# Deformable sampling beside the attention: one bilinear corner moves from VectorE to ScalarE, and the output convolution takes two tiles at once

## The chip, the cores and the metric

One NeuronCore of a Trainium2 chip runs the whole program. The time is the device time of one execution in microseconds, and of several executions the median counts.

## What is computed

The input is x, four samples of 128 channels by 64 x 64 pixels in fp32. Four layers follow one another, each of the form x = x + layer(group_norm(x)).

```python
# layer 0: attention over the L = 4096 pixels of a sample (keys and values are the same)
q, k = Wq @ xf + bq, Wk @ xf + bk
attn = softmax(q.T @ k / sqrt(128));  out = xf + attn @ k.T
# layer 1: weights of 9 taps made from x by two small matmuls, times the dilated taps of x
# layer 2: 7x7 depthwise convolution, layer norm, 128 -> 512 -> 128 with gelu
# layer 3: deformable convolution, 9 taps
offset, mask = conv3x3(x)                       # 18 offsets, 9 masks for each pixel
py, px = y + dy_k + offset_y, x + dx_k + offset_x
val = c00*(1-ly)*(1-lx) + c01*(1-ly)*lx + c10*ly*(1-lx) + c11*ly*lx   # 4 gathered corners
out = relu(batch_norm(einsum('bckhw,ock->bohw', val * mask, weight)))
```

Layer 3 is what the change touches: for every pixel and each of the 9 taps, four corners of 128 channels are gathered, weighted and added, and the 9 sums go through a matmul with 9 weight matrices of 128 x 128.

## The kernel before, in words

**Samples and stages.** A sample is a tile of 128 channels by 4096 pixels in SBUF. `sample(n, dcn)` runs, on each engine's own queue, the group norm, `attention`, `layer1`, `layer2` and `layer3_prepare`. The deformable sampling of sample n-1 isn't done in its own turn: it is woven into the attention of sample n (`dcn` is true for n = 1, 2, 3). That of the last sample runs alone at the end (`tail_*`).

**Attention.** The 4096 queries are cut into 8 chunks of 512 (`NCH`), the 4096 keys into 32 tiles of 128 (`T`), which makes 256 steps (`STEPS`). In step `at` each engine does its piece, in this order in its queue:

- TensorE: `scores(at + 2)`, four matmuls of 512 columns in bf16 (lines 485 to 488) into one of two banks, once `exp_done` says that the bank has been read; `weigh_values(at - 1)`, twelve matmuls of 129 columns (line 519), the last four of them after VectorE and GpSimd have made the low part of the exponentials (`pl_v`, `pl_p`); `max_scores` for a later chunk, one matmul of 512 columns (line 446) into one of two banks, once VectorE has reduced the bank's former content (`mx_red`). The last 38 steps have no `max_scores`.
- ScalarE: `exponent(at)` (line 838).
- VectorE: `low_values(at + 1)` (line 1237) for 320 of 512 columns, then `max_reduce` (line 1177).
- GpSimd: `low_values(at + 1)` (line 1589) for the other 192 columns, then the gathers.

Once for each chunk TensorE also has `q_project` (line 409), `input_rows` (line 471) and `shift_rows` (line 457), and VectorE has `normalize` (lines 1192, 1198), `input_sum` (line 1186), `q_low` (line 1157) and `max_finish` (lines 1162 to 1166).

**Sampling.** The 4096 pixels are 32 tiles of 128. Tile j begins at step `begin(j) = 15 * j // 2`, so there is one tile in 7.5 steps, and `tile_at(at, offset)` gives the tile that is `offset` steps old. Nine indirect DMAs (line 1578, GpSimd) in steps -12 to -6 bring the patches: for each tap 4 corners x 128 channels for 128 pixels. The patches of a tile lie in one of four slots (`patches`: two in `G`, one in `regq`, one in `x_cur`, with a ninth tap of the latter two in `xl`). Then, by offset:

- 1 to 3, ScalarE `first_corner` (line 854): `val = corner 0 * weight`, nine instructions of 128 elements. 4 to 6, `second_corner` (line 862): corner 1 is scaled in its own place.
- 3 to 8, VectorE `interpolate`, 18 `scalar_tensor_tensor` (line 1214), three in a step: `val += corner 2 * weight`, then `val += corner 3 * weight`. 9: one addition of the whole tile, `val += corner 1` (line 1224, and line 1227 for the ninth tap in two slots of four), a drain, and `val_rdy`. `val` has two halves, by j % 2.
- 11 to 13, TensorE `dcn_transposes` (line 533), three in a step, into columns 0 to 383 of bank `TR[0]`. The first group waits for `val_rdy`, the others for `tr_ev`, which says that the group before has been copied out. 13 to 15, ScalarE `dcn_evacuate` (line 869), 384 columns. ScalarE runs about two steps ahead of TensorE, since `exponent(at)` needs only `scores(at)`.
- 14 to 16, TensorE `dcn_conv` (line 542), three of nine fp32 matmuls in a step, each with 128 columns, into columns 384 to 511 of the same bank. In the profile an fp32 matmul of this kind is two records. 18, ScalarE `dcn_result` (line 876); 20, for every fourth tile VectorE `dcn_finish` (line 1250) and a store.

The functions that the change touches follow, with the line numbers of the profile.

## Time and profile before

| | us |
|---|---|
| median of 3 runs (4402.11 to 4411.94) | 4408.24 |
| the profiled execution | 4407.83 |
| its span, first to last instruction | 4406.1 |

The page gives the busy time of each engine, the chain of work that ended last, and groups of instructions by line. The timeline lists single instructions with their starts. A record of a matmul is longer than the time to the next start, as matmuls are pipelined, so costs are taken from start to start. "PEld" is the weight load of TensorE. An "x3" after a row of the timeline says that three equal instructions are merged, and "[0.80 <- DVEq L1228]" that the engine sat idle for 0.80 us before this instruction, until VectorE's queue reached line 1228. Of the TensorE matmul rows a few per cent are missing, of the weight loads none that matters here.

### The profile page before, as it was taken

How to read it: one execution, taken by the hardware profiler on the slowest of the kernel's cores; microseconds unless marked ns; L12 is line 12 of the kernel's file. 1: busy time of each engine (PE TensorE's matmuls, PEld its weight loads, DVE VectorE, ACT ScalarE, POOL GpSimd, SP SyncE). 2: the span in 40 equal slices, each digit the busy share in tenths (PEclk: the TensorE clock that was granted, in tenths of full speed). 3: DMA queues.
4: the chain of work that ended last, by engine and by line, in shares of the span. 5: the costliest groups of instructions: out<-in, count | busy, mean ns of one | idle time of the engine just before them, and what ended most of it. 6: DMA issues, size and time to landing. Idle time of an engine off the chain costs nothing.

```text
span 4406.1 us, 76129 instructions
## 1 busy us (share of the span) xinstructions
PE 3694.5 (84%) x25784; PEld 2322.8 (53%) x26161; DVE 3455.3 (78%) x7009; ACT 2026.8 (46%) x4605; POOL 2220.1 (50%) x2457
## 2 busy tenths in 40 slices
PE   4999789879999869969999968978999977984555
PEld 2666434347776624436777733434777753433444
DVE  5999687579999768759999957848999967854666
ACT  2444432346666541236666742235666653222333
POOL 3444340058878550028877732007888834004775
PEclk9999899889999979989999988988999988986565
DMA  1000100154545300045554400034454520006775
GB/s 46 11 11 11 27 1 0 46 155 149 157 146 155 96 0 1 0 141 152 153 154 146 134 25 1 0 93 141 150 155 149 152 62 0 0 19 186 216 222 178
DMA packets 206462, 401.41 MB, mean 91 GB/s; under 512 B 23089, under 2 KB 121804, under 8 KB 204584
## 3 DMA queue, kind: packets, MB, share of 16 engines
q0 software_dynamic: 92160, 302.06, 22.9%
q1 hardware_dynamic: 113906, 94.92, 7.3%
q8 instruction: 197, 3.23, 0.3%
q14 instruction: 145, 1.19, 0.1%
q10 hardware_dynamic: 54, 0.01, 0.0%
HBM read 337.36 MB, written 59.53 MB: 90 GB/s over the span
## 4 chain that ended last, share of the span: by engine, by line
PE 44%; DVE 25%; issue 11%; POOL 10%; POOLq 4%; DVEq 3%; ACT 2%; DMA 1%; SPq 0%; ACTq 0%; another core or an unknown queue 0%
PE bank L657 11%; PE bank L519 8%; DVE val L1214 8%; DVE mxc L1177 6%; DVE xl L1237 4%; POOL G L1578 3%; DVE val L1224 2%; PE bank L683 2%; POOLq L1553 2%; PE bank L699 2%; PE bank L486 2%; PE bank L542 2%; PE bank L720 2%; PE bank L722 2%; PE bank L446 1%
## 5 line engine op out<-in xcount | busy, mean ns | idle before, releaser
L1589 POOL TENSOR_TENSOR xl<-pt 128x192 bf16<-128x192 f32 (+1 forms) x1024 | 683.4, 668 | 441.2 <-ACT pt L838 215.2
L838 ACT ACTIVATE pt<-bank 128x512 f32<-128x512 f32 x1024 | 608.8, 595 | 574.4 <-PE bank L488 317.3
L1578 POOL DMA_INDIRECT G<-patch_table,idx x576 | 590.9, 1026 | 202.5 <-issue 114.3
L519 PEld LDWEIGHTS bank<-vt,pt 128*128 128x128 bf16 x8192 | 549.5, 98 | 242.8 <-ACT pt L838 3.9
L1177 DVE TENSOR_REDUCE mxc<-bank 128x1 f32<-128x512 f32 x896 | 608.1, 680 | 38.0 <-PE bank L446 31.7
L519 PE MATMUL bank<-vt,pt 128*128 128x129 bf16 (+1 forms) x8192 | 633.7, 220 | 3.5 <-ACT osb L846 1.6
L1360 DVE SCALAR_TENSOR_TENSOR G<-xn,vec,G 128x512 f32<-128x512 f32 x736 | 521.6, 748 | 47.2 <-issue 40.7
L1237 DVE TENSOR_TENSOR xl<-pt 128x320 bf16<-128x320 f32 (+1 forms) x1024 | 500.1, 489 | 73.0 <-PE bank L519 53.8
L1563 POOL TENSOR_TENSOR rs<-ve,mhalf 128x4 f32<-128x4 f32 x32 | 36.6, 1143 | 820.1 <-ACT ve L974 820.1
L519 PE MATMUL bank<-vt,xl 128*128 128x129 bf16 x4096 | 401.7, 221 | 12.3 <-DVE xl L1237 11.6
L657 PE MATMUL bank<-vt,val 128*128 (+1 forms) x1152 | 373.2, 389 | 19.5 <-DVE xl L1152 19.5
L1214 DVE SCALAR_TENSOR_TENSOR val<-G,w,val 128x128 f32<-128x128 f32 x864 | 317.6, 419 | 4.4
L1578 POOL DMA_INDIRECT x_cur<-patch_table,idx x256 | 273.7, 1069 | 56.9 <-issue 48.4
L486 PE MATMUL bank<-ql,regk 128*128 128x512 bf16 x768 | 292.9, 381 | 5.0 <-issue 0.5
L487 PE MATMUL bank<-qh,regk 128*128 128x512 bf16 x762 | 290.8, 382 | 0.0
L1578 POOL DMA_INDIRECT regq<-patch_table,idx x256 | 258.7, 1011 | 61.7 <-issue 45.7
L519 PEld LDWEIGHTS bank<-vt,xl 128*128 128x128 bf16 x4096 | 273.4, 98 | 18.5 <-DVE xl L1237 16.7
L446 PE MATMUL bank<-regk,qh 128*128 128x512 bf16 x711 | 272.2, 384 | 12.5 <-DVE mxc L1177 9.3
L488 PE MATMUL bank<-m,ones 128*128 128x512 bf16 x738 | 281.5, 381 | 0.3
L485 PE MATMUL bank<-qh,regk 128*128 128x512 bf16 x678 | 258.5, 381 | 5.1 <-ACT m L817 2.3
L542 PE MATMUL bank<-valt,dcnw_s 128*128 128x128 f32 x1728 | 242.4, 276 | 1.6
L542 PEld LDWEIGHTS bank<-valt,dcnw_s 128*128 128x128 f32 x1728 | 233.9, 191 | 8.5 <-issue 1.5
(253 smaller groups left out, 7247.6 us busy)
## 6 DMA issues: line engine op xcount, KB each, us to landing
patch_table<-valt SPq DMA_DIRECT2D x64, 512.0 KB, 7.1
G<-patch_table,idx POOLq DMA_INDIRECT x576
x_cur<-in_x SPq DMA_DIRECT2D x4, 2048.0 KB, 8.4
xl<-in_x SPq DMA_DIRECT2D x32, 256.0 KB
attn_out<-ob SPq DMA_DIRECT2D x32, 256.0 KB
x_store<-x_cur SPq DMA_DIRECT2D x4, 2048.0 KB, 6.3
xr<-x_store SPq DMA_DIRECT2D x32, 256.0 KB, 4.6
out<-fo SPq DMA_DIRECT2D x32, 256.0 KB
```

The lines of the kernel that those rows point to most:

```text
L446: mm(MX[at % 2], qh[:, q0:q0 + 128], kh[:, mc * CH:(mc + 1) * CH], start=True, stop=True)\
L486: mm(bank, kh[:, tile], cols(ql, i % Q_RING), start=False, stop=False)
L519: last = mm(O[t // 2][:, c0:c0 + width], image[:, at % ring, t * 128:(t + 1) * 128], vhl[:, values, st, 0:width], start=(st == 0 and part ...
L542: last = mm(TR[0][:, 384:512], dcnw_s[:, k, :], valt[:, k, piece], start=(k == 0), stop=(k == K1 - 1))
L657: last = mm(as_rows(ST[u][:]), diag(k, part), shifted(c, k // 7 - 3, k % 7 - 3, image), start=(k == 0 and image is xh and part == 0), stop ...
L838: A(pt[:, at % PT_RING, :], ST[at % ST_RING] if n else ST_FIRST[at % 3], ACT.Exp, scale=SCALE).then_inc(s["exp_done"], 1)
L1177: v.reduce_max(mxc[:, t, mc:mc + 1], MX[at % 2], AX.X).then_inc(s["mx_red"], 1)
L1214: v.scalar_tensor_tensor(dst, src, w4[:, j, corner * K1 + k:corner * K1 + k + 1], dst, ALU.mult, ALU.add)
L1237: v.tensor_tensor(pl[:, at % PL_RING, first:CH], pt[:, at % PT_RING, first:CH], ph[:, at % PT_RING, first:CH], ALU.subtract).then_inc(s["p ...
L1360: v.scalar_tensor_tensor(acc, src, wgt, acc, ALU.mult, ALU.add)
L1578: g.indirect_dma_start(out=patches(j, k), out_offset=None, in_=table[:], in_offset=bass.IndirectOffsetOnAxis(ap=idx[:, j * K1 + k:j * K1 + ...
L1589: g.tensor_tensor(pl[:, at % PL_RING, 0:stop], pt[:, at % PT_RING, 0:stop], ph[:, at % PT_RING, 0:stop], ALU.subtract).then_inc(s["pl_p"], 1)
```

## The change

Nine more instructions of ScalarE scale corner 2 in its own place, as corner 1 is scaled already (`corner_scale`, which spreads 27 instructions over offsets 1 to 8). VectorE keeps nine `scalar_tensor_tensor` for corner 3 (offsets 4 to 6) and does two whole-tile additions, of corner 1 at offset 7 and of corner 2 at offset 9, each behind a wait (`c1_rdy`, `c2_rdy`) and a drain. The transposes come in five groups of two, two, two, two and one (offsets 11 to 15) into columns 0 to 255 of the bank, and each is evacuated by an instruction of 256 or 128 columns (offsets 13 to 17). The convolution runs for odd tiles alone, for both tiles of the pair, with 256 columns: five of the nine matrices at offset 16, four at offset 17. Its result is read at offset 19, `dcn_finish` comes at 21. The counters of the tail are renumbered, with nothing else changed there; those parts are left out.

```diff
@@ -41,7 +41,8 @@
 PATCH = 4 * C
 SCALE = float(C) ** -0.5
 STEPS = NCH * T
-SPT = 7
+SPT = 5
+TRR = 5
 X_COPY, X_ROWS, X_SUM = 10, 12, 13
 Q_NEXT, SHIFT = 18, 28
 LEAD, LEAD_FIRST = 6, 10
@@ -265,7 +266,7 @@
             "t_ps t_ev in_ve in_pow in_ready relu_rdy tl_rdy l1w l1p l1s l1a l1f "
             "diag_rdy dwp y_rdy ln_m ln_d ln_sq ln_v ln_ve ln_rs ln_dg ln_bc z_rdy hp gl mo me xa "
             "oc_ps oc_ev ot_ps ot_ev xs_rdy xt_ps xt_ev om_rdy em_rdy grid_rdy idx_rdy x3_out tbl_w "
-            "gat0 gat1 gat2 gat3 c1_rdy val_rdy tr_ps tr_ev conv_ps res_rdy xr_in fin fin_out tail_ps").split()}
+            "gat0 gat1 gat2 gat3 c1_rdy c2_rdy val_rdy tr_ps tr_ev conv_ps res_rdy xr_in fin fin_out tail_ps").split()}
 
         weights = ((wq_s[:], wq), (wk_s[:], wk), (l2w1_s[:], l2w1), (l2w2_s[:], l2w2), (offw_s, offw),
                    (offb_s[:], offb), (dcnw_s[:], dcnw), (vec[:], vecs))
@@ -382,7 +383,7 @@
         @block.tensor
         def _(pe):
             mm = nc.tensor.matmul
-            pe.sem_inc(s["tr_ps"], 4)
+            pe.sem_inc(s["tr_ps"], TRR + 1)
             for name in ("mo", "xt_ps", "ot_ps"):
                 pe.sem_inc(s[name], 2)
             pe.wait_ge(s["w_in"], 16 * WEIGHTS)
@@ -525,24 +526,25 @@
                 J = m * T + j
                 if r == 0:
                     pe.wait_ge(s["val_rdy"], J + 1 + 2)
-                    if j:
+                    if j and j % 2 == 0:
                         pe.wait_ge(s["res_rdy"], J)
-                else:
-                    pe.wait_ge(s["tr_ev"], 3 * J + r + 1)
-                for k in range(3):
-                    last = nc.tensor.transpose(TR[0][:, k * 128:(k + 1) * 128], val[:, j % 2, 3 * r + k, :],
+                if r or j % 2:
+                    pe.wait_ge(s["tr_ev"], TRR * J + r + 1)
+                for k in range(2 * r, min(2 * r + 2, K1)):
+                    last = nc.tensor.transpose(TR[0][:, k % 2 * 128:(k % 2 + 1) * 128], val[:, j % 2, k, :],
                                                ident[:])
                 last.then_inc(s["tr_ps"], 1)
 
             def dcn_conv(m, j, r):
-                piece = slice(j % TB * 128, (j % TB + 1) * 128)
+
+                piece = slice((j % TB - 1) * 128, (j % TB + 1) * 128)
                 if r == 0:
-                    pe.wait_ge(s["tr_ev"], 3 * (m * T + j + 1) + 1)
-                for k in range(3 * r, 3 * r + 3):
-                    last = mm(TR[0][:, 384:512], dcnw_s[:, k, :], valt[:, k, piece],
+                    pe.wait_ge(s["tr_ev"], TRR * (m * T + j + 1) + 1)
+                for k in range(5 * r, min(5 * r + 5, K1)):
+                    last = mm(TR[0][:, 256:512], dcnw_s[:, k, :], valt[:, k, piece],
                               start=(k == 0), stop=(k == K1 - 1))
-                if r == 2:
-                    last.then_inc(s["conv_ps"], 1)
+                if r == 1:
+                    last.then_inc(s["conv_ps"], 2)
 
             def attention(n, dcn):
                 lag = 5 if dcn else 2
@@ -590,12 +592,13 @@
                     if not dcn and r == IMAGE and i + 1 < NCH:
                         image_of_shift(i + 1)
                     if dcn:
-                        for part in range(3):
+                        for part in range(TRR):
                             j = tile_at(at, 11 + part)
                             if j is not None:
                                 dcn_transposes(n - 1, j, part)
-                            j = tile_at(at, 14 + part)
-                            if j is not None:
+                        for part in range(2):
+                            j = tile_at(at, 16 + part)
+                            if j is not None and j % 2:
                                 dcn_conv(n - 1, j, part)
                 weigh_values(n, STEPS - 1)
 
...
@@ -845,36 +848,31 @@
                 for h in range(2):
                     A(osb[:, h, :], O[h][:, 0:2 * (C + 1)], ACT.Copy).then_inc(s["o_evac"], 1)
 
-            def first_corner(m, j, part):
-
-                if part == 0:
-                    act.wait_ge(s["tr_ps"], 3 * (m * T + j) + 1)
+            def corner_scale(m, j, o):
+
+                corner, k = o // K1, o % K1
+                if o == 0:
+                    act.wait_ge(s["tr_ps"], TRR * (m * T + j) + 1)
                     act.wait_ge(gathered(j), landed(m, j))
-                for k in range(3 * part, 3 * part + 3):
-                    last = A(val[:, j % 2, k, :], patches(j, k)[:, 0:C], ACT.Copy, scale=w4[:, j, k:k + 1])
-                if part == 2:
-                    last.then_inc(s["c0_rdy"], 1)
-
-            def second_corner(m, j, part):
-
-                for k in range(3 * part, 3 * part + 3):
-                    src = patches(j, k)[:, C:2 * C]
-                    last = A(src, src, ACT.Copy, scale=w4[:, j, K1 + k:K1 + k + 1])
-                if part == 2:
-                    last.then_inc(s["c1_rdy"], 1)
+                src = patches(j, k)[:, corner * C:(corner + 1) * C]
+                op = A(val[:, j % 2, k, :] if corner == 0 else src, src, ACT.Copy,
+                       scale=w4[:, j, corner * K1 + k:corner * K1 + k + 1])
+                if k == K1 - 1:
+                    op.then_inc(s[f"c{corner}_rdy"], 1)
 
             def dcn_evacuate(m, j, r):
-                act.wait_ge(s["tr_ps"], 3 * (m * T + j) + r + 1 + 4)
+                act.wait_ge(s["tr_ps"], TRR * (m * T + j) + r + 1 + TRR + 1)
                 piece = slice(j % TB * 128, (j % TB + 1) * 128)
-                A(valt[:, 3 * r:3 * r + 3, piece], TR[0][:, 0:384].rearrange("p (k n) -> p k n", k=3), ACT.Copy)\
-                    .then_inc(s["tr_ev"], 1)
+                taps = min(2, K1 - 2 * r)
+                A(valt[:, 2 * r:2 * r + taps, piece],
+                  TR[0][:, 0:taps * 128].rearrange("p (k n) -> p k n", k=taps), ACT.Copy).then_inc(s["tr_ev"], 1)
 
             def dcn_result(m, j):
                 act.wait_ge(s["conv_ps"], m * T + j + 1)
-                if j % TB == 0:
+                if j % TB == 1:
                     act.wait_ge(s["fin_out"], 16 * (m * NCH + j // TB + 1))
-                A(fo[:, j % TB * 128:(j % TB + 1) * 128], TR[0][:, 384:512], ACT.Relu, bias=bn[:, 3:4],
-                  scale=bn[:, 2:3]).then_inc(s["res_rdy"], 1)
+                A(fo[:, (j % TB - 1) * 128:(j % TB + 1) * 128], TR[0][:, 256:512], ACT.Relu, bias=bn[:, 3:4],
+                  scale=bn[:, 2:3]).then_inc(s["res_rdy"], 2)
 
             def attention(n, dcn):
                 def values(c):
@@ -912,18 +910,16 @@
                     if not dcn and r == IMAGE + 1 and i + 1 < NCH:
                         image_copy(i + 1)
                     if dcn:
-                        for part in range(3):
+                        for part in range(TRR):
                             j = tile_at(at, 13 + part)
                             if j is not None:
                                 dcn_evacuate(n - 1, j, part)
-                            j = tile_at(at, 1 + part)
+                        for o in range(3 * K1):
+                            j = tile_at(at, 1 + 5 * o // 18)
                             if j is not None:
-                                first_corner(n - 1, j, part)
-                            j = tile_at(at, 4 + part)
-                            if j is not None:
-                                second_corner(n - 1, j, part)
-                        j = tile_at(at, 18)
-                        if j is not None:
+                                corner_scale(n - 1, j, o)
+                        j = tile_at(at, 19)
+                        if j is not None and j % 2:
                             dcn_result(n - 1, j)
                 values_evacuate(n, NCH - 1)
 
...
@@ -1204,27 +1200,25 @@
 
                 if r == 0:
                     dve.wait_ge(s["c0_rdy"], m * T + j + 1)
-                if r < SPT - 1:
-                    for o in range(3 * r, 3 * r + 3):
-                        corner, k = 2 + o // K1, o % K1
-                        if corner > 2 and k == 0:
-                            dve.drain()
-                        src = patches(j, k)[:, corner * C:(corner + 1) * C]
+                if r < 3:
+                    for k in range(3 * r, 3 * r + 3):
                         dst = val[:, j % 2, k, :]
-                        v.scalar_tensor_tensor(dst, src, w4[:, j, corner * K1 + k:corner * K1 + k + 1], dst,
-                                               ALU.mult, ALU.add)
+                        v.scalar_tensor_tensor(dst, patches(j, k)[:, 3 * C:4 * C], w4[:, j, 3 * K1 + k:3 * K1 + k + 1],
+                                               dst, ALU.mult, ALU.add)
                 else:
-                    dve.wait_ge(s["c1_rdy"], m * T + j + 1)
+                    q = r - 2
+                    dve.wait_ge(s[f"c{q}_rdy"], m * T + j + 1)
                     dve.drain()
                     slot = j % TB
                     joint = K1 if slot < 2 else K1 - 1
                     held = G[:, slot] if slot < 2 else (regq, x_cur)[slot - 2][:, 0:joint * PATCH]\
                         .rearrange("p (k e) -> p k e", e=PATCH)
                     dst = val[:, j % 2, 0:joint, :]
-                    v.tensor_tensor(dst, dst, held[:, :, C:2 * C], ALU.add)
+                    v.tensor_tensor(dst, dst, held[:, :, q * C:(q + 1) * C], ALU.add)
                     if joint < K1:
                         dst = val[:, j % 2, joint, :]
-                        v.tensor_tensor(dst, dst, patches(j, joint)[:, C:2 * C], ALU.add)
+                        v.tensor_tensor(dst, dst, patches(j, joint)[:, q * C:(q + 1) * C], ALU.add)
+                if r == SPT - 1:
                     dve.drain()
                     dve.sem_inc(s["val_rdy"], 1)
 
@@ -1284,10 +1278,10 @@
                         q_low(n, i + 2)
                     if dcn:
                         for part in range(SPT):
-                            j = tile_at(at, 3 + part)
+                            j = tile_at(at, (4, 5, 6, 7, 9)[part])
                             if j is not None:
                                 interpolate(n - 1, j, part)
-                        j = tile_at(at, 20)
+                        j = tile_at(at, 21)
                         if j is not None and j % TB == TB - 1:
                             dcn_finish((n - 1) * NCH + j // TB)
                 normalize(n, NCH - 1, 0)
```

## Rows read from the trace of the kernel before

**Rows 1.** Windows: the first attention with sampling, and a stretch inside it.

```profile
core 0: us, PE busy (x) PEld busy (x) DVE busy (x) ACT busy (x) POOL busy (x), PEclk, DMA share, GB/s
951.00:1530.00 579.00, 555.23 (x5160) 408.38 (x5254) 537.58 (x1181) 391.56 (x998) 455.47 (x532) 1.00 0.48 143
...
1000.00:1450.00 450.00, 432.10 (x3994) 318.93 (x4066) 436.49 (x961) 309.08 (x795) 370.71 (x432) 1.00 0.51 153
```

**Rows 2.** Chain of waits by line, 951 to 1530 us (the answer ends there).

```profile
by line: DVE val L1214 20.6%; DVE mxc L1177 14.1%; DVE xl L1237 10.4%; PE bank L519 10.1%; issue 7.6%; DVE val L1224 5.9%; PE bank L486 3.7%; PE bank L542 3.4%; PE bank L487 3.2%; PE bank L488 3.2%; PE bank L485 2.8%; PE bank L533 2.5%; DVE
```

**Rows 3.** Line 486, one load a step: attentions 1 and 3.

```profile
L486 PEld LDWEIGHTS bank<-ql,regk x256: 95/98/152, 951.8 to 1525.9; 128*128 128x128 bf16 x128
L486 PEld LDWEIGHTS bank<-ql,regk x256: 96/98/147, 3020.3 to 3594.0; 128*128 128x128 bf16 x128
```

**Rows 4.** Timeline of TensorE, first attention with sampling: start us, us, what.

```profile
1101.54 0.38 PE L485 MATMUL bank<-qh,regk 128*128 128x512 bf16 x1
...
1103.62 0.38 PE L485 MATMUL bank<-qh,regk 128*128 128x512 bf16 x1
...
1106.06 0.38 PE L485 MATMUL bank<-qh,regk 128*128 128x512 bf16 x1
...
1112.67 0.38 PE L485 MATMUL bank<-qh,regk 128*128 128x512 bf16 x1
...
1114.43 0.38 PE L485 MATMUL bank<-qh,regk 128*128 128x512 bf16 x1
```

**Rows 5.** Timeline of TensorE in layer 2: fp32 records of 512 columns.

```profile
699.69 1.88 PE L683 MATMUL bank<-valt,l2w_s 128*128 128x512 f32 x4
701.40 0.38 PE L657 MATMUL bank<-vt,val 128*128 x1
```

**Rows 6.** Waits of the weight loads, 951 to 1530: us, times, longest.

```profile
PEld bank L533 <- DVEq L1228: 18.1, 20, 1.7
PEld bank L446 <- DVE mxc L1177: 5.4, 13, 1.1
```

**Rows 7.** Timeline of VectorE: three in a step; a whole-tile addition; a chunk end.

```profile
1118.09 1.14 DVE L1214 SCALAR_TENSOR_TENSOR val<-G,w,val 128x128 f32<-128x128 f32 x3
1119.15 0.48 DVE L1237 TENSOR_TENSOR xl<-pt 128x320 bf16<-128x320 f32 x1
...
1120.15 1.14 DVE L1214 SCALAR_TENSOR_TENSOR val<-G,w,val 128x128 f32<-128x128 f32 x3
...
1130.36 0.48 DVE L1237 TENSOR_TENSOR xl<-pt 128x320 bf16<-128x320 f32 x1
...
1131.54 1.36 DVE L1224 TENSOR_TENSOR val<-val,G 128x1152 f32<-128x1152 f32 x1
1133.09 0.49 DVE L1237 TENSOR_TENSOR xl<-pt 128x320 bf16<-128x320 f32 x1 [0.20 <-issue]
...
1161.40 0.19 DVE L1162 TENSOR_REDUCE mx<-mxc 128x4 f32<-128x32 f32 x1
...
1162.27 0.49 DVE L1166 SCALAR_TENSOR_TENSOR mhl<-mx,mhl 128x4 bf16<-128x4 f32 x1
```

**Rows 8.** Timeline of ScalarE: scalings, an exponential, copies of 258 columns.

```profile
1100.03 0.97 ACT L862 ACTIVATE G<-G,w 128x128 f32<-128x128 f32 x3
1100.91 0.58 ACT L838 ACTIVATE pt<-bank 128x512 f32<-128x512 f32 x1
1101.39 0.66 ACT L846 ACTIVATE osb<-bank 128x258 f32<-128x258 f32 x2
1101.92 0.50 ACT L869 ACTIVATE valt<-bank 128x384 f32<-128x384 f32 x1
```

**Rows 9.** Waits of ScalarE, 951 to 1530 us.

```profile
ACT pt L838 <- PE bank L488: 105.8, 181, 2.2
```

**Rows 10.** Group of GpSimd, 1000 to 1450 us, and what it waited for.

```profile
L1589 POOL TENSOR_TENSOR xl<-pt 128x192 bf16<-128x192 f32 x196 | 120.1, 613 | 31.9 <-PE bank L519 23.0 <-ACT pt L838 5.8
```

**Rows 11.** Timeline of GpSimd: an issue beside the addition of rows 7.

```profile
1131.73 2.00 POOL L1578 DMA_INDIRECT G<-patch_table,idx  x1
```

More of the change, by code:

```diff
@@ L762, in tail_transposes @@
                 for r in range(3):
-                    pe.wait_ge(s["tr_ev"], 3 * (TAIL + j) + r - 2 + 1)
+                    pe.wait_ge(s["tr_ev"], TRR * TAIL + 3 * j + r - 2 + 1)
                     for k in range(3):
@@ L771, in tail_conv @@
                 q, t = j // TB, j % TB
-                pe.wait_ge(s["tr_ev"], 3 * (TAIL + j + 1) + 1)
+                pe.wait_ge(s["tr_ev"], TRR * TAIL + 3 * (j + 1) + 1)
                 if t == 0 and q >= 2:
@@ L1031, in tail_corner @@
                 act.wait_ge(gathered(j), landed(N - 1, j))
-                act.wait_ge(s["tr_ps"], 3 * (TAIL + j) + 1)
+                act.wait_ge(s["tr_ps"], TRR * TAIL + 3 * j + TRR - 2)
                 for k in range(K1):
```

2 lines of the change are left out of this document (1 added, 1 removed).

## The prediction

> **What bounds the kernel now.** I read the windows first: in the three attentions with sampling TensorE is busy for 555 of 579 us and VectorE for 538, ScalarE for 392, GpSimd for 455 [rows 1]. The reader is to see that two engines are nearly full and two are not; the clock is at its higher level, 2.4 GHz, throughout. Busy shares can't say which of the two sets the pace, so next comes the chain of waits: more than half of it is VectorE (lines 1214, 1177, 1237, 1224 alone 51%), the rest mostly TensorE [rows 2]. It suggests that VectorE's work is the price. The third view says how much of it can be had. One weight load of line 486 comes in each step; from the first to the last of them the first and the third attention take 574.1 and 573.7 us [rows 3], and the second is as long. What would TensorE need if it never waited? A step without sampling takes 1.76 us, one with three transposes 2.08, one with six records of the convolution 2.44 [rows 4]. So a transpose costs 0.107 us, a convolution record 0.113.
>
> - 256 steps x 1.76 = 450.6
> - no maxima in the last 38: -38 x 0.214 = -8.1 (half of an fp32 record of 512 columns, which takes (701.40 - 699.69) / 4 = 0.428 [rows 5])
> - 288 transposes x 0.107 = 30.8
> - 32 tiles x 18 records x 0.113 = 65.1
> - matmuls once a chunk (12 fp32 records of 512 columns, some 60 small transposes): 12 x 0.428 + 60 x 0.107 = 11.6
>
> Together 550.0. The stall is therefore 24 us for each attention, 72 in all. A view of its own agrees: the weight loads waited 18.1 us for VectorE's queue after line 1228 (`val_rdy`) and 5.4 for the maxima [rows 6]. This is the centre of my argument: TensorE stands close under VectorE, so only 72 us can come from unloading VectorE, however much is unloaded.
>
> **VectorE.** Removed: nine of line 1214 in a tile. Three of them take 1119.15 - 1118.09 = 1.06 us to the next start, so 3.18. Added: one whole-tile addition. A step without sampling is 1120.15 - 1119.15 = 1.00, one with the present addition 1133.09 - 1130.36 = 2.73, so this costs 1.73 with its two drains [rows 7]; the new one has one drain, and I take 1.5 (1.36, its bare duration, to 1.73). Net 1.7 us less in a tile (1.45 to 1.8). In the stretch from 1000 to 1450 us, 26 tiles' worth and 195 steps, VectorE is busy for 436.5 [rows 1] and has drains in most of the rest, so its need is 448 at most; after the change 448 - 26 x 1.7 = 404. TensorE's floor there is 195 x 1.76 + 26 x (9 x 0.107 + 18 x 0.113) + some 10 = 431. VectorE falls from 104% of it to 94%.
>
> **TensorE, convolution.** 36 records of 128 columns for a pair become 18 of 256. The trace has none of 256. From rows for 128 (0.113) and 512 columns (0.428) a straight line gives 0.218, the ends are half of 0.428 (0.214) and twice 0.113 (0.226). A pair then takes 3.92 instead of 4.07: 0.15 x 16 pairs x 3 = 7 us (0 to 10). I take 6. The transposes are the same nine.
>
> **What is late next.** The pair's convolution makes two steps of 1.76 + 10 x 0.218 = 3.9 and 3.5 us, and leaves thirteen of 1.76 to 1.98. VectorE rests in the long ones and starts the short ones without lag. In these its steps are 1.0 without sampling, 2.1 with three of line 1214, 2.5 at offset 7, 1.0 at offset 8 and 2.7 at offset 9. When it is caught up, the reduction of step 9 starts about 1.9 after TensorE began that step, and `val_rdy` comes with the reduction and the addition behind it, 0.6 + 1.7 later, at 4.2. TensorE wants it at two steps plus 1.76, so at 5.3 to 5.7. The margin is 1.0 to 1.4 us. Offset 7 uses up 0.5 of it, which offset 8 gives back; what exceeds it is the work of once a chunk, of which the end of the maxima alone is 1162.76 - 1161.40 = 1.36 [rows 7]. I let each of 24 chunks still cost 0.75 us: 18 us of stall remain (6 to 40).
>
> **ScalarE.** 27 scalings in a tile instead of 18, at (1100.91 - 1100.03) / 3 = 0.293: +2.64. Evacuation: a copy of 258 columns takes (1101.92 - 1101.39) / 2 = 0.265 [rows 8], so four of these and a shorter one are 1.2, against three of 384 columns at about 0.38, 1.15. In all +2.6 x 32 = 83 us on 392 busy of 579. It is hidden: ScalarE waits 105.8 us for scores in one attention [rows 9]. Queued behind the five evacuations are the exponentials. In such a step: copy 0.27, four scalings 1.17, exponential 0.48, together 1.92, against 1.98 of TensorE; the step with five scalings takes 2.2, but is single. An exponential is needed two TensorE steps after its scores, so ScalarE can be late by some 1.5 us before anyone waits. Cost nothing; if the cover is gone, see below. The waits `c1_rdy` and `c2_rdy` lie behind scalings of offsets 4, 5 and 8, in a queue two steps ahead of VectorE's 7 and 9: nothing. The result read at 19 and the finish at 21 delay a store by one step, of which the next needs nothing for 15: nothing. No DMA is added or moved; the tail is as before.
>
> **GpSimd.** It is busy for 370.7 of 450 us and waits 28.8 for others before line 1589 [rows 10]; the rest is issue time and waits of the gathers. I put its need at 410. An addition of VectorE stretches what runs beside it: an issue that began 0.2 us into one took 2.00 us, the additions taking 1.36 [rows 7, 11]. The price of one more lies between 0 and 1.36; I take 0.5, as only some instructions of GpSimd meet it: 410 + 13 = 423, still under 431. The Trainium skill (page "SBUF — State Buffer", the section on the two sides of SBUF) says that a VectorE instruction with two SBUF inputs holds the port pair shared with GpSimd as an exclusive lock for its whole length, and the other fully blocks. Rows 11 agree in kind; if this held at full length for each addition, the sum would be that of the third case below.
>
> **Sum.** -72 + 18 - 6 = -60. The profiled execution took 4407.83 and the median is 4408.24, so both bases give **4348 us**.
>
> **The rivals.**
> - *TensorE's floor* (the forecast): 0.62. Between 4408 - 78 = 4330 with no stall left and 4370 with 40 us of it.
> - *VectorE's bursts keep paying*: with the convolution bunched, VectorE idles in the long steps and is chased in the short ones, where its mean is 2.1 against 1.9 to 2.0 of TensorE. For it: the present stall sits in exactly that wait [rows 6]. Against it: the margin above. Half to nearly all of the stall stays: 4408 - 6 - 10 to 36 = 4366 to 4392. Chance 0.25.
> - *GpSimd's port*: each added addition costs it its whole 1.36 us. Need 410 + 35 = 445 of the present 450: nothing to win in the steps with gathers, 4400, no measurable change. Against it: nine two-input instructions go at the same time, and most gathers are stretched by less. Chance 0.07.
> - *ScalarE's handshakes* (slower): transposes of group r wait until group r-1 is copied out, now four times in a tile instead of twice. If ScalarE ran late by more than 1.3 us in that stretch, every handshake would stand open on the path. At 0.3 us for each of 5 x 96 = 480 groups that is 144 us, less the 78 gained: 4474; at 0.2, 4426. It decides from 0.16 us a group on. Against it: 105.8 us of waiting that ScalarE has to spare [rows 9]. Chance 0.06.
>
> **How the numbers follow.** A measurement of this kernel can tell about 0.2%, 9 us. The first two cases are faster by more: 0.87. The third is no change: 0.07. The fourth is slower: 0.06. Range 4328 to 4390: it takes in the first case whole, the second nearly, and leaves out the last two.
>
> **What would show it.** Right: the loads of line 486 span 555 to 560 us in each attention; the wait of line 533 for line 1228 falls from 18 to under 7 us; the chain of waits is mostly TensorE; records of line 542 start 0.21 to 0.22 apart; ScalarE is busy for some 470 us and still waits for scores. Wrong: records of line 542 further apart; line 533 waiting for line 869; GpSimd's issues of 2 us twice in a tile and TensorE waiting for line 1589; VectorE idle before its additions, for ScalarE.

## The result: no gain, and the profile after

| us | before | after |
|---|---|---|
| median, same chip, 11 runs each | 4408.24 (4402.11 to 4415.35) | 4416.94 (4411.95 to 4418.98) |
| ratio, 95% interval | | 1.0018 [1.0009, 1.0026] |
| span of the profiled execution | 4406.1 | 4415.3 |

The forecast was 4348. The kernel became no faster; it is slower by 9 us, which is just about what can be told. Most lines after the edit have moved by one to six: line 533 (transposes) is 534, 542 (convolution) 544, 838 (exponential) 841, 869 (evacuation) 867, 1228 (`val_rdy`) 1222, 1177 (maxima) 1173, 1589 (GpSimd's low part) 1583. All scalings are line 858.

The windows of after, in the stretches and columns of [rows 1]:

```profile
951.00:1530.00 579.00, 558.17 (x4919) 389.58 (x4919) 491.45 (x941) 458.23 (x1331) 471.32 (x531) 1.00 0.48 143
1000.00:1450.00 450.00, 437.02 (x3847) 306.28 (x3845) 400.53 (x772) 364.22 (x1069) 383.39 (x430) 1.00 0.51 152
```

VectorE lost 36 of 436 us in the inner stretch, as meant, and ScalarE took 55 more. But GpSimd, whose program was not touched, is busy for 383.4 instead of 370.7 us. The length of an attention, by the load that comes once in a step:

```profile
L487 PEld LDWEIGHTS bank<-ql,regk x256: 96/98/151, 952.8 to 1530.0; 128*128 128x128 bf16 x128
```

577.2 us, and 577.6 and 576.8 in the other two, against 574.1, 575.7 and 573.7 before (the first and the last are in [rows 3]). In what follows, "attention" is this length for the first one.

The waits after, 951 to 1534 us, ScalarE's and then those of the weight loads (us, times, longest):

```profile
ACT val L858 <- PE bank L534: 42.9, 30, 2.3
ACT pt L841 <- PE bank L489: 36.7, 69, 3.2
...
PEld bank L544 <- ACT valt L867: 13.9, 15, 1.5
PEld bank L486 <- ACT pt L841: 7.0, 22, 0.5
PEld bank L534 <- DVEq L1222: 3.4, 3, 1.7
```

TensorE's wait for `val_rdy` fell from 18.1 [rows 6] to 3.4 us. In its place TensorE waits for ScalarE, for evacuations and for exponentials. And ScalarE has a wait that wasn't there: 42.9 us, 30 times, for transposes, ahead of a *scaling*. VectorE is no longer chased; between 1000 and 1450 it waits 35 us for TensorE, where before there was under one:

```profile
L1173 DVE TENSOR_REDUCE mxc<-bank 128x1 f32<-128x512 f32 x195 | 133.1, 683 | 35.3 <-PE bank L447 34.7
```

The timeline of ScalarE after, around one such wait:

```profile
1108.85 1.28 ACT L858 ACTIVATE val<-G,w 128x128 f32<-128x128 f32 x4 [1.03 <-PE bank L534]
1110.03 0.39 ACT L858 ACTIVATE G<-G,w 128x128 f32<-128x128 f32 x1
1110.33 0.57 ACT L841 ACTIVATE pt<-bank 128x512 f32<-128x512 f32 x1
1110.80 0.26 ACT L867 ACTIVATE valt<-bank 128x128 f32<-128x128 f32 x1
```

and TensorE in the same stretch:

```profile
1108.54 0.27 PE L534 MATMUL bank<-ident,val 128*128 128x128 f32 x1
...
1111.11 2.43 PE L544 MATMUL bank<-valt,dcnw_s 128*128 128x256 f32 x10 [0.54 <-ACT valt L867]
...
1115.13 1.89 PE L544 MATMUL bank<-valt,dcnw_s 128*128 128x256 f32 x8
1116.86 0.38 PE L486 MATMUL bank<-qh,regk 128*128 128x512 bf16 x1
```

The first scaling of tile j writes the half of `val` that tile j - 2 used. Its wait, unchanged in form, asks for all transposes of tile j - 2. With three groups these ended at offset 13 of that tile; with five they end at offset 15, which is offset 0 of tile j. ScalarE reaches offset 1 two steps ahead of TensorE, so it now stands still until the ninth transpose is done (1108.54). Behind it are queued five scalings (four of this tile, one of the tile before), the exponential and the fifth evacuation, which starts at 1110.80; the convolution, which needs that evacuation, starts at 1111.11 after 0.54 us of waiting.

### The profile page after: what moved, and what is told of

Read it like the earlier page. It is cut to its first block and busy times, and to the rows that moved or that the text cites. A ratio compares the mean times of both kernels' runs of the same rounds, so it can differ in the third digit from the quotient of the medians.

```text
span 4415.3 us, 75090 instructions
## 1 busy us (share of the span) xinstructions
PE 3712.7 (84%) x25297; PEld 2268.4 (51%) x25297; DVE 3323.4 (75%) x6289; ACT 2229.9 (51%) x5613; POOL 2279.7 (52%) x2457
## 5 line engine op out<-in xcount | busy, mean ns | idle before, releaser
L1583 POOL TENSOR_TENSOR xl<-pt 128x192 bf16<-128x192 f32 (+1 forms) x1024 | 726.3, 711 | 396.5 <-ACT pt L841 268.9
L447 PE MATMUL bank<-regk,qh 128*128 128x512 bf16 x896 | 341.3, 382 | 9.8 <-DVE mxc L1173 6.6
L486 PE MATMUL bank<-qh,regk 128*128 128x512 bf16 x768 | 293.2, 382 | 7.9 <-ACT m L820 4.0
L1572 POOL DMA_INDIRECT regq<-patch_table,idx x256 | 267.9, 1046 | 56.4 <-issue 50.6
L488 PE MATMUL bank<-qh,regk 128*128 128x512 bf16 x768 | 292.5, 381 | 0.0
L489 PE MATMUL bank<-m,ones 128*128 128x512 bf16 x768 | 292.3, 381 | 0.0
L858 ACT ACTIVATE G<-G,w 128x128 f32<-128x128 f32 x864 | 281.9, 395 | 0.0
L544 PE MATMUL bank<-valt,dcnw_s 128*128 128x256 f32 x864 | 207.5, 385 | 27.8 <-ACT valt L867 27.8
L660 PE MATMUL bank<-xl,val 128*128 (+1 forms) x576 | 224.4, 390 | 0.0
```

The source lines that it names most:

```text
L447: mm(MX[at % 2], qh[:, q0:q0 + 128], kh[:, mc * CH:(mc + 1) * CH], start=True, stop=True)\
L486: mm(bank, kh[:, tile], cols(qh, i % Q_RING), start=True, stop=False)
L488: mm(bank, kl[:, tile], cols(qh, i % Q_RING), start=False, stop=False)
L660: last = mm(as_rows(ST[u][:]), diag(k, part), shifted(c, k // 7 - 3, k % 7 - 3, image), start=(k == 0 and image is xh and part == 0), stop ...
L1572: g.indirect_dma_start(out=patches(j, k), out_offset=None, in_=table[:], in_offset=bass.IndirectOffsetOnAxis(ap=idx[:, j * K1 + k:j * K1 + ...
L1583: g.tensor_tensor(pl[:, at % PL_RING, 0:stop], pt[:, at % PT_RING, 0:stop], ph[:, at % PT_RING, 0:stop], ALU.subtract).then_inc(s["pl_p"], 1)
```

## The experiments

Seventeen kernels ran, in five sets; each ratio is to the kernel before on the same chip, with its 95% interval. The runs were spread over several chips, on which the kernel before took 4407 to 4411 us; so where times of two runs are subtracted, some 4 us can come from the chips. Three theories stood at first for the wait in place of VectorE's: A, the first scaling's wait for the transposes takes ScalarE's lead; B, the convolution stands too close behind the last evacuation; C, 27 scalings are too much for ScalarE.

**1. corners_later**: the scalings two steps later, so that the transposes of tile j - 2 are done.

```diff
-                            j = tile_at(at, 1 + 5 * o // 18)
+                            j = tile_at(at, 3 + 5 * o // 18)
```

> The changed kernel with all 27 scalings two steps later (offsets 3 to 10 instead of 1 to 8), nothing else. Theory A (lost lead): the first scaling of tile j writes the half of val that tile j-2 used, and so waits for its fifth group of transposes, which TensorE issues only at offset 0 of tile j; ScalarE at offset 1, two steps ahead, stands still for up to 1.5 us in each tile (42.9 us in the first attention) and loses the lead that hides its 27 scalings. Then this run gives 4345 to 4365 us: the wait of line 858 for line 534 is gone, that of the convolution for the last evacuation (13.9 us in the first attention) too. Theory B (the convolution is put one step too close to the last evacuation, whatever the scalings do): no change, 4410 to 4420. Theory C (27 scalings are too much for ScalarE): 4400 to 4415.

4384.45 us (4382.14 to 4386.13), ratio 0.995 [0.9936, 0.9964], attention 567.9. The wait of line 858 and the convolution's wait for the evacuation are gone from the trace. The 32 us are A's, but they are half of what was missing, and the time lies 19 us above the range that was given for A.

**2. conv_later**: the convolution, and what follows it, one step later.

```diff
-                            j = tile_at(at, 16 + part)
+                            j = tile_at(at, 17 + part)
...
-                        j = tile_at(at, 19)
+                        j = tile_at(at, 20)
...
-                        j = tile_at(at, 21)
+                        j = tile_at(at, 22)
```

> The changed kernel with the pair's convolution at offsets 17 and 18, its result at 20 and the finish at 22, nothing else. Theory A (lost lead): the convolution no longer waits, 12 times 0.7 us less in an attention at most, but ScalarE stays late and exponentials and evacuations are late instead: 4390 to 4412. Theory B (only the distance from evacuation to convolution is wrong): all of the 13.9 us in an attention come back, and little else is lost: 4370 to 4380. Theory C (too much for ScalarE): 4405 to 4415.

4405.42 us (4398.48 to 4408.66), ratio 0.9998 [0.9989, 1.0007], attention 574.9. This is in A's range, and just inside C's. The largest wait of the weight loads, same stretch as above:

```profile
PEld bank L486 <- ACT pt L841: 17.4, 37, 0.8
```

The convolution's 13.9 us are gone and the scores wait for exponentials 10 us longer; ScalarE's 42.6 us ahead of line 858 stay. B named where ScalarE's lateness was paid, not where it came from.

**3. corner_alone**: the kernel before with the third corner on ScalarE alone; transposes in three groups, convolution of 128 columns.

```diff
-SPT = 7
+SPT = 5
...
-                            j = tile_at(at, 1 + part)
-                            if j is not None:
-                                first_corner(n - 1, j, part)
-                            j = tile_at(at, 4 + part)
+                        for o in range(3 * K1):
+                            j = tile_at(at, 1 + 5 * o // 18)
                             if j is not None:
-                                second_corner(n - 1, j, part)
+                                corner_scale(n - 1, j, o)
...
-                            j = tile_at(at, 3 + part)
+                            j = tile_at(at, (4, 5, 6, 7, 9)[part])
```

> The kernel before with the corner part of the change alone: 27 scalings at offsets 1 to 8 on ScalarE, nine of line 1214's kind and two whole-tile additions on VectorE; transposes in three groups (offsets 11 to 13) and the convolution tile by tile as before. Theory A (lost lead): the transposes of tile j-2 end two steps before the first scaling of tile j, so ScalarE keeps its lead and TensorE comes near its floor of 550 us in each attention: 4350 to 4370. Theory C (27 scalings are too much for ScalarE): 4400 to 4415. If unloading VectorE is worth nothing: 4400 to 4410.

4376.59 us (4373.87 to 4377.94), ratio 0.9933 [0.992, 0.9947], attention 563.5. It falls in none of the three ranges: faster than C and the last allow, 7 us slower than A's.

**4. pair_alone**: the change without its corner part; five groups and the convolution of two tiles stay.

```diff
-SPT = 5
+SPT = 7
...
-                        for o in range(3 * K1):
-                            j = tile_at(at, 1 + 5 * o // 18)
+                        for part in range(3):
+                            j = tile_at(at, 1 + part)
+                            if j is not None:
+                                first_corner(n - 1, j, part)
+                            j = tile_at(at, 4 + part)
                             if j is not None:
-                                corner_scale(n - 1, j, o)
+                                second_corner(n - 1, j, part)
```

> The changed kernel with the interpolation of the kernel before (18 scalings on ScalarE at offsets 1 to 6, 18 two-input instructions and one addition on VectorE), so five groups of transposes and the convolution of two tiles alone. Theory A (lost lead): the first scaling waits for the fifth group here too, but nine fewer scalings let ScalarE catch up; VectorE is as full as before and bunched convolutions help it little: 4405 to 4435. Theory C (too much for ScalarE in the changed kernel): 4400, as before less the 6 us of the wider convolution.

4402.87 us (4395.02 to 4410.05), ratio 0.999 [0.9981, 0.9999], attention 572.8. This is 2 us below A's range and 3 above C's figure. Its ScalarE stands still for the transposes as long as in the change (45.7 us), but with 18 scalings it makes up most of it: the convolution waits for the last evacuation for 5.0 us in the attention, where the change has 13.9, and scores for exponentials for 0.2, where the change has 7.0 us. Together, 3 and 4 say: the parts alone give -31 and -4 us, both give +9. So the wait costs far more where the third corner has taken ScalarE's slack. What it costs in pair_alone isn't shown, as no run gave that kernel the finer wait. C falls with 3: the same 27 scalings, without the late transposes, are in a faster kernel.

**5. fine_wait**: the change, but each second scaling waits only for the transposes that read its part of `val`.

```diff
                 corner, k = o // K1, o % K1
+                if corner == 0 and k % 2 == 0:
+                    act.wait_ge(s["tr_ps"], max(1, TRR * (m * T + j) - 3 + k // 2))
                 if o == 0:
-                    act.wait_ge(s["tr_ps"], TRR * (m * T + j) + 1)
```

> The changed kernel with every instruction at its place; only the wait of the first scalings is cut up: instead of waiting at tap 0 until all five groups of transposes of tile j-2 are through, taps 0 and 1 wait for its first group, taps 2 and 3 for the second, and so on (tap 8 for the fifth). Theory A (the lost lead comes from this one wait): line 858 no longer waits for line 534, the convolution no longer waits for the last evacuation, the exponentials are early again: 4370 to 4388, as with the scalings moved by two steps (4384). If the two steps helped for another reason (a better spread of the ScalarE's work): 4405 to 4418.

4384.89 us (4382.45 to 4389.88), ratio 0.9946 [0.9932, 0.996], attention 567.0. The largest wait of its ScalarE:

```profile
ACT pt L841 <- PE bank L489: 48.8, 74, 3.2
```

No scaling waits any more, and the time is that of run 1, reached another way and within A's range. A is shown, at 32 us. It leaves 4385 against 4348.

**6. no_third_corner**: the kernel before without the nine instructions for corner 2. No work stands in their place anywhere.

```diff
-                    for o in range(3 * r, 3 * r + 3):
+                    for o in range(max(3 * r, K1), 3 * r + 3):
```

> The kernel before without the nine instructions of line 1214 for corner 2, which is left out of the interpolation; nothing is put in their place. So VectorE loses 3.2 us in a tile, GpSimd sees no added two-input addition of 1152 columns, ScalarE does what it did. If my arithmetic of TensorE's floor is right (550 us in an attention) and GpSimd is what keeps the corner part at 564 us: 550 to 554 us in an attention, 4338 to 4352. If a floor of another kind holds (something stalls TensorE beside VectorE and GpSimd): 4365 to 4380, like the corner part alone (4377).

4341.2 us (4339.27 to 4342.86), ratio 0.9844 [0.983, 0.9857]:

```profile
L486 PEld LDWEIGHTS bank<-ql,regk x256: 96/98/147, 952.8 to 1504.0; 128*128 128x128 bf16 x128
```

551.2 us: TensorE's floor, worked out at 550.0, is right. So the gain was there to be had; corner_alone, at 563.5, misses 12 us of it in each attention. What corner_alone has and this one hasn't is the second whole-tile addition and nine more scalings on ScalarE; run 14 (corner_gp128) reaches 551.0 with the same scalings and less work on GpSimd, so the scalings by themselves don't cost the 12 us. The windows of corner_alone and then of no_third_corner (951 to 1530), and corner_alone's group of GpSimd (1000 to 1450), against [rows 1, 10]:

```profile
951.00:1530.00 579.00, 553.56 (x5165) 409.42 (x5258) 507.44 (x951) 466.19 (x1286) 481.35 (x533) 0.99 0.50 145
...
951.00:1530.00 579.00, 551.16 (x5170) 410.43 (x5264) 454.61 (x915) 396.50 (x1002) 437.09 (x534) 0.98 0.50 145
```

```profile
L1579 POOL TENSOR_TENSOR xl<-pt 128x192 bf16<-128x192 f32 x200 | 143.2, 719 | 3.3
```

GpSimd does the same instructions in 481.4 us instead of 455.5, each low part in 719 ns instead of 613, and it hardly waits ahead of them any more: 3.3 us where there were 31.9. In its place TensorE waits: in corner_alone the matmuls of the low part (951 to 1534 us) stand still for GpSimd for 6.1 us, before for 0.7, in no_third_corner not at all.

```profile
L519 PE MATMUL bank<-vt,xl 128*128 128x129 bf16 x1024 | 100.1, 220 | 6.9 <-POOL xl L1579 6.1
```

With no_third_corner the 26 us between the kernel before and corner_alone come apart. The nine instructions that leave VectorE give GpSimd 455.5 - 437.1 = 18.4 us back, 0.57 us a tile. What corner_alone has besides takes 481.4 - 437.1 = 44.3 us, 1.38 a tile, where the whole-tile additions last 1.40 on average when they are 1152 wide. Summed over the 256 low parts and 273 issues of each of the three attentions, these are 0.35 and 1.24 us a tile. No run has the addition alone, without the nine scalings.

**7, 8. corner_pool128, corner_pool160**: corner_alone with 128 or 160 of the 512 low-part columns on GpSimd instead of 192; VectorE takes the rest.

```diff
-PL_POOL, PL_POOL_FIRST, PL_RING = 192, 352, 3
+PL_POOL, PL_POOL_FIRST, PL_RING = 128, 352, 3
```

> The corner part alone (4377) with GpSimd taking 128 columns of the low part instead of 192 and VectorE 384 instead of 320. GpSimd's busy time rose from 453 to 479 us in an attention with the added addition, VectorE's fell to 502. If GpSimd's lateness is what remains (14 us over the floor in an attention): GpSimd loses some 0.1 us in a step and the time is 4352 to 4366. If what remains is VectorE's bursts, the 0.07 us more in each of its steps cost: 4380 to 4395.

> The same with 160 and 352 columns. If GpSimd's lateness is what remains: 4360 to 4372, between the corner part alone and the run with 128 columns. If VectorE's bursts are: 4377 to 4386.

4342.92 us (4337.64 to 4343.6), ratio 0.9845 [0.9831, 0.9858], attention 552.6; and 4360.41 (4355.47 to 4364.72), 0.9883 [0.9868, 0.9899], attention 557.2. The first is 9 us better than even the range for GpSimd's lateness, the second at the lower end of it. Work put *onto* VectorE makes the kernel 34 us faster, and half of it about half as much.

**9. before_pool128**: the same line in the kernel before, where the chain of waits was mostly VectorE.

> The kernel before with GpSimd taking 128 columns of the low part instead of 192 and VectorE 384, nothing else: the control for the run of 4343 us. There VectorE sets the pace, so 256 steps x 0.07 us x 3 attentions make it slower: 4440 to 4470. If it is 4400 or less, the gain from 4377 to 4343 came from the split itself and not from the additions that stretch GpSimd's work.

4363.57 us (4360.98 to 4369.35), ratio 0.9906 [0.9891, 0.9922], attention 559.7. The expectation was wrong by 76 us or more and in its sign, and this is the run that taught most. Its groups, VectorE and then GpSimd, 1000 to 1450:

```profile
L1237 DVE TENSOR_TENSOR xl<-pt 128x384 bf16<-128x384 f32 x201 | 117.7, 586 | 5.6 <-issue 4.5 <-PE bank L519 0.6 <-ACT pt L838 0.6
L1214 DVE SCALAR_TENSOR_TENSOR val<-G,w,val 128x128 f32<-128x128 f32 x237 | 79.0, 385 | 1.2
```

```profile
L1589 POOL TENSOR_TENSOR xl<-pt 128x128 bf16<-128x128 f32 x201 | 104.2, 518 | 30.3 <-PE bank L519 23.7 <-ACT pt L838 3.5
```

and the two of VectorE before:

```profile
L1237 DVE TENSOR_TENSOR xl<-pt 128x320 bf16<-128x320 f32 x194 | 104.8, 540 | 5.4 <-issue 4.5 <-PE bank L519 0.7 <-ACT pt L838 0.2
L1214 DVE SCALAR_TENSOR_TENSOR val<-G,w,val 128x128 f32<-128x128 f32 x219 | 79.0, 412 | 1.1
```

VectorE pays 46 ns a step for 64 more columns, 7.5 x 0.046 = 0.35 us in a tile, and gets back 18 x 0.027 = 0.49 on line 1214, whose work is the same (18 x 0.035 = 0.63 with the patches of the other slots, where it falls further, from 420 to 385 ns over all). GpSimd gains 95 ns a step. The instructions of line 1214 had been stretched by GpSimd running beside them. The net of a tile makes some 9 us of the 14.4 that the attention became shorter; the rest isn't taken apart. Run 16 shows the stretching with VectorE's program untouched: with 64 columns less on GpSimd, line 1214 takes 382 ns instead of 412 and the low part of 320 columns 516 instead of 540.

**10. after_pool128, 11. fine_pool128**: the same line in the change, and in run 5.

> The changed kernel with 128 columns on GpSimd. Two causes were found: ScalarE's lost lead (worth 31 us, 4417 to 4385) and GpSimd's lateness (worth 34 us on the corner part alone, 4377 to 4343). If they are independent: 4380 to 4390. If the lost lead hides GpSimd's lateness, since both are waits of the same engine at the same time: 4395 to 4410, and most of the gain of the split comes only with the cut-up wait.

> The changed kernel with both causes taken away: the wait of the first scalings cut up by tap, and 128 columns on GpSimd. If these two are all that failed in the prediction: 4338 to 4350, at TensorE's floor of 548 us in an attention. If the bunched convolution leaves VectorE and TensorE chasing each other: 4352 to 4370.

4402.4 us (4400.05 to 4405.1), ratio 0.9989 [0.998, 0.9998], attention 573.3, ScalarE still waiting 42.3 us ahead of line 858; and 4351.83 (4351.27 to 4352.53), ratio 0.9875 [0.986, 0.9891], attention 556.2. The first is in its second range, the second between its two. So with the finer wait alone -32, with the smaller share of GpSimd alone -15, with both -65 (by the ratios -32, -13 and -63): each hides part of the other. The chain of waits of fine_pool128, 951 to 1530, to be held against [rows 2]:

```profile
by line: PE bank L520 23.9%; PE bank L544 10.9%; PE bank L487 8.0%; PE bank L489 7.7%; PE bank L488 7.6%; PE bank L486 7.5%; PE bank L534 5.8%; PE bank L447 4.6%; issue 3.6%; DVE mxc L1174 2.3%; ACT val L859 2.0%; DVE val L1207 1.7%; DVE xl
```

**12. fine_pool128_spread**: run 11 with the convolution in three steps of three matrices (offsets 16 to 18).

```diff
-                for k in range(5 * r, min(5 * r + 5, K1)):
+                for k in range(3 * r, 3 * r + 3):
```

> The same with the pair's convolution in three steps of three matrices (offsets 16, 17, 18; result at 20, finish at 22) instead of five and four in two steps. If bunching costs: 4338 to 4345, and 5 to 15 us less than with two steps. If it doesn't: the same within 5 us.

4358.27 us (4356.53 to 4360.26), ratio 0.989 [0.9875, 0.9905], attention 558.0. Neither range holds it. Run 11 is 9 us above run 7, its like without the pair, and run 5 is 8 above run 3 (by the ratios 13 and 6), though the pair should save 6. Spreading makes it 6 us worse, so bunched matmuls aren't the reason. The traces of runs 7 and 11 (951 to 1510 us) tell where it is lost: TensorE waits 0.6 us for `val_rdy` in run 7 and 4.1 in run 11, and 1.6 and 2.5 for the maxima. They also hold a candidate that no run tested: ScalarE reads the pair's result at offset 19, in a queue two steps ahead of TensorE's 17, and stands still before it for 14.9 us in the attention of run 11 (8.2 of them for TensorE), for 2.2 in that of run 7. The cause stays open.

**13 to 16. corner_ve256, corner_gp128, before_ve256, before_gp128**: who needs the relief? In corner_alone and in the kernel before, 64 columns of the low part are left out altogether, once on VectorE (it starts at 256) and once on GpSimd (128 columns, VectorE still starts at 192).

```diff
-                first = PL_POOL if n else PL_POOL_FIRST
+                first = 256 if n else PL_POOL_FIRST
```

> The corner part alone (4377) with VectorE making 256 columns of the low part instead of 320; GpSimd keeps its 192, and 64 columns are left out of the sum. It relieves VectorE alone. If GpSimd's own lateness is what the corner part still pays: 4370 to 4378. If it is VectorE, stretched by the port that it shares with GpSimd: 4350 to 4362, as VectorE has 0.067 us less in each step.

> The corner part alone with GpSimd making 128 columns instead of 192 and VectorE still 320; 64 columns are left out of the sum. If GpSimd's lateness is what the corner part pays: 4340 to 4346, the same as with VectorE taking over the 64 (4343). If VectorE mattered too: 4 to 10 us below that run.

> The kernel before with VectorE making 256 columns of the low part instead of 320, GpSimd 192 as before, 64 left out of the sum. If VectorE sets the pace of the kernel before, as its chain of waits says: 0.067 us x 256 steps x 3 attentions = 51 us less, 4355 to 4375. If GpSimd does: 4400 to 4408.

> The kernel before with GpSimd making 128 columns instead of 192 and VectorE still 320, 64 left out of the sum. With VectorE taking the 64 over it was 4364. If the gain of that run is time that GpSimd's instructions had held VectorE up by, this one wins more, since VectorE's share doesn't grow: 4338 to 4350. If GpSimd alone had been late: 4360 to 4366.

| from | VectorE 64 less | GpSimd 64 less | moved to VectorE |
|---|---|---|---|
| corner_alone, 4376.59, ratio 0.9933 | 4346.74, 0.9854 [0.9839, 0.9869] | 4340.67, 0.984 [0.9827, 0.9854] | 4342.92, 0.9845 |
| before, 4410.67 | 4375.84, 0.9914 [0.9901, 0.9928] | 4348.12, 0.9858 [0.984, 0.9876] | 4363.57, 0.9906 |

Less on either engine helps, in both kernels: neither alone was the bound. In both, GpSimd's 64 columns are worth more than VectorE's, 62 against 35 us in the kernel before (36 against 30 in corner_alone, where TensorE's floor ends the gain), and moving them is worth GpSimd's gain less a little that VectorE takes on (62 - 18 = 44, and 36 - 2 = 34). One of the four executions of before_gp128 took 9741 us, which nothing here explains; 4348.12 is the median of the other three. The two runs with less on GpSimd are in their first ranges; corner_ve256 is 3 us faster than its second range, before_ve256 1 us slower than its first. The attention of corner_gp128 is 551.0, the floor again.

**17. corner_pool96**: run 7 with 96 columns on GpSimd.

> The corner part alone with GpSimd making 96 columns of the low part and VectorE 416. With 192, 160 and 128 columns it took 4377, 4360 and 4343, and at 128 an attention takes 552 us against TensorE's floor of 550. If the floor binds from here on: 4338 to 4346. If VectorE's share now costs more than GpSimd's relief gives: 4348 to 4360.

4339.84 us (4337.64 to 4341.92), ratio 0.9841 [0.9827, 0.9854]. It is in the first range, computes everything, is 1.6% faster than the kernel before and faster than the change, and stands at TensorE's floor, with an attention of 551.1 us.

## Why the prediction was wrong

- **What bounds the kernel now**: half right. TensorE's floor of 550.0 us is confirmed by three kernels at 551.0 to 551.2, so some 70 us were there. (The length from the first load to the last holds 255 steps, not 256; counted so, the sum gives 548.2, 3 us under the measured floor.) "It suggests that VectorE's work is the price" was half the truth: less of it does help (35 us in run 15), but GpSimd had stretched VectorE's instructions (412 against 385 ns on line 1214), and the work of the two together was the price, as runs 9 and 13 to 16 show. Taking VectorE's busy 436.5 us as its own need was the error.
- **VectorE**: right in kind. Its load fell by 36 us in the stretch, against 26 x 1.7 = 44, and it ended up waiting. The added addition takes 1.42 us bare, where 1.36 to 1.73 was allowed.
- **TensorE, convolution**: right. The next start after eight records comes (1116.86 - 1115.13) / 8 = 0.216 us each, against 0.218. Whole steps agree: over plain steps of 1.76 us, the six of 2.43 us in which run 7 convolves two tiles cost 4.0 us, the two of 3.92 and 3.49 us of run 11 cost 3.9, so a pair saves 0.12 us, 6 us in all. In the complete kernel they can't be seen: pair_alone gives 4 us, and on top of the third corner the pair costs 8 to 9 us even with both causes mended.
- **What is late next** looked only at VectorE's margin. The sum left 18 us of stall for three attentions, 6 in each; at `val_rdy` the first one has 3.4. The sign "falls from 18 to under 7" thus came true while the time didn't: the path had moved to ScalarE.
- **ScalarE**: the step that failed first. "Cost nothing" was argued from 105.8 us of waiting ahead of the exponentials [rows 9] and from steps of 1.92 against 1.98 us, and the waits checked were the new ones. The unchanged wait at the head of `corner_scale` was not: the change moved its releaser, the last transposes, from offset 13 to 15. ScalarE's total of busy time was well forecast (458 for "some 470"). The price is 32 us by runs 1 and 5, and it falls due in full only where the third corner has filled ScalarE's slack: pair_alone has 45.7 us of the same standing still, and its convolution waits 5.0 us, not 13.9. The rival *ScalarE's handshakes* named the right engine, but priced another wait, the handshake between groups, at 18 to 66 us of loss; that one came to 0.2 us in the attention, while the convolution, whose wait nobody had priced, waited 13.9 us for the last evacuation.
- **GpSimd**: the second step that failed. "I take 0.5" was for one more addition, and the nine instructions that go were put at nothing. The net of both measured 0.81 us a tile, (481.4 - 455.5) / 32, and no_third_corner takes it apart: about 1.38 (1.24 over three attentions) for what is added, less 0.57 (0.35) for what is gone. So the term was mis-sized, and that the net came as near to 0.5 as it did is luck. Then "410 + 13 = 423, still under 431" compared GpSimd with TensorE as if waiting 28.8 us meant 28.8 us to spare. In corner_alone that wait is gone and 12 us of each attention with it, and moving 64 columns off GpSimd gives 34 us back. The rival *GpSimd's port* had the price of an addition right (1.36 us) and its outcome wrong (4400, where corner_alone took 4377), since it too left out what the nine give back. The Trainium skill (page "SBUF — State Buffer", the section on the two sides of SBUF) states the lock between VectorE and GpSimd as one by which the other fully blocks; for a VectorE instruction with two SBUF inputs it says so only against a GpSimd instruction that reads SBUF. The traces agree that each holds up the other, and in size too: 1.2 to 1.4 us for an addition of some 1.4. The lock itself no trace shows.
- **Sum.** Of 69 us between 4417 and 4348, the finer wait and GpSimd's share return 65 together: 4352, in the range, with TensorE on the chain. Neither of the two was in the sum.
- **What would show it**: under "wrong" stood "line 533 waiting for line 869" and "GpSimd's issues of 2 us twice"; the first came true in another form: the transposes wait for the evacuation for 0.2 us, the convolution for 13.9.

What stays open: why the paired convolution costs 8 to 9 us in a kernel whose other causes are removed, and which part of 1.38 us is the addition's alone.

## What to carry to other kernels

When a change splits a step into more groups or moves it, look up every wait in the program on the semaphore that it signals, the unedited ones too, and compare the releaser's new place with how far ahead the waiting engine runs: a queue that is two steps ahead meets a buffer-reuse wait two steps early. When the chain of waits runs through VectorE while GpSimd is some 80% busy with SBUF work, compare the mean duration of one VectorE form with its shortest before calling VectorE the bound; here giving VectorE 64 *more* columns and GpSimd 64 fewer was worth 44 us by itself. A wait that came with a part which alone made the kernel 4 us faster cost 32 us beside another part that uses up the same slack, so measure the parts and the whole. And when a change swaps instructions, price what the removed ones had cost the other engines as well as what the added ones will.

## What the runs showed of the hardware that was not expected

- GpSimd and VectorE slow each other. In the kernel before, between 1000 and 1450 us, GpSimd's instructions that overlap one of the 26 whole-tile additions by more than 0.1 us were compared with the others, one by one: an indirect DMA's issue took 1.28 us on average (34 of them) against 1.03, a low part of 192 columns 1.07 (11 of them) against 0.59. So a single instruction is on average held up for less than the addition's length, but nearly two meet each addition, and the low part is nearly doubled. The others aren't undisturbed either: most of them overlap shorter two-input instructions of VectorE.
- VectorE's reduction that reads a bank in PSUM doesn't follow GpSimd's load: 679 ns in the kernel before, 678 with 128 columns on GpSimd, 680 in corner_alone, 683 after. Its instructions with SBUF inputs are: 412 to 385 ns.
- An fp32 matmul record of 256 columns costs 0.216 us, half of one of 512 columns (0.428 [rows 5]), and a record of 128 columns 0.113: within 5% in proportion to the columns.
